# A two-layer decoder on one core: the gate rides in the routed row, the last join is shared by three engines, and four early weight loads are issued between others

## The reference, cut to what matters

```python
logits = xf @ gate_w + gate_b
probs = softmax(logits)
gates, expert_idx = top_k(probs, 2)
h = relu(einsum('nc,ech->neh', xf, w1) + b1)           # 256 -> 512, per expert
expert_out = einsum('neh,ehc->nec', h, w2) + b2        # 512 -> 256
out = sum over a token's two experts of gate * expert_out
x = layernorm(x + out)
```

## Time and profile before

| | us |
|---|---|
| median of 3 runs | 1017.17 |
| lowest and highest | 1013.34, 1018.77 |
| the profiled execution | 1013.71 |
| its span in the trace | 1011.9 |
| PE busy in the span | 896.4 (89%) |
| DVE, ACT, POOL busy | 624.8, 483.8, 282.7 |

### The profile page before, as it was taken

How to read it: one execution, slowest core, us unless ns; L and a number is a source line. 1 busy time by engine, 2 the same in 40 slices (tenths; PEclk the granted TensorE clock), 3 DMA queues, 4 the chain that set the end, 5 groups by cost and what they waited for, 6 DMA issues and landing times.

```text
span 1011.9 us, 20131 instructions
## 1 busy us (share of the span) xinstructions
PE 896.4 (89%) x7498; PEld 717.1 (71%) x7498; DVE 624.8 (62%) x1836; ACT 483.8 (48%) x1123; POOL 282.7 (28%) x432
## 2 busy tenths in 40 slices
PE   3669999999997989999999999999999998698980
PEld 2446778768776757677777878687878897597870
DVE  4999886684663898867746778787543632014006
ACT  2335546344555545464545646644446543243430
POOL 4323322221420344312211333333311322124222
PEclk9679999999998989999999999999999999799995
DMA  9999000000010000000000032213111479797944
GB/s 319 405 324 313 8 1 12 11 2 16 32 32 7 17 27 28 17 6 11 12 11 12 28 111 76 73 38 127 53 58 48 136 220 327 274 345 271 383 186 163
DMA packets 39426, 114.88 MB, mean 114 GB/s; under 512 B 5465, under 2 KB 21601, under 8 KB 38689
## 3 DMA queue, kind: packets, MB, share of 16 engines
q1 hardware_dynamic: 35584, 103.35, 29.6%
q0 software_dynamic: 3744, 10.24, 2.7%
HBM read 99.13 MB, written 37.59 MB: 135 GB/s over the span
## 4 chain that ended last, share of the span: by engine, by line
PE 67%; DVE 14%; ACT 5%; DMA 5%; issue 5%; SPq 2%; POOL 1%; POOLq 0%; ACTq 0%; DVEq 0%
PE ps L693 47%; PE ps L698 8%; PE ps L705 6%; PE ps L769 3%; DMA xs_d<-X,idx 2%; ACT PT L1415 1%; DVE PT L1097 1%; DMA EW<-moe_w 1%; ACT slot_rows L1415 1%; PE ps L836 1%; DVE stat L1033 1%; DVE slot_rows L1338 1%; PE ps L994 1%; PE ps L870 1%; DMA slot_rows<-ys_d 1%
## 5 line engine op out<-in xcount | busy, mean ns | idle before, releaser
L1586 POOL TENSOR_TENSOR stat<-stat,mhalf 128x1 f32<-128x1 f32 x112 | 65.7, 586 | 305.6 <-DVE stat L1035 305.5
L693 PE MATMUL ps<-wall,slot_rows 128*128 128x256 f32 (+1 forms) x448 | 134.7, 427 | 10.0 <-ACT KB L1442 8.5
L693 PEld LDWEIGHTS ps<-wall,slot_rows 128*128 128x128 f32 x448 | 79.3, 194 | 32.7 <-issue 21.3
L1097 DVE TENSOR_REDUCE PT<-ps 128x8 f32<-128x1024 f32 x64 | 75.3, 1219 | 24.5 <-PE ps L705 24.5
L705 PEld LDWEIGHTS ps<-KB 32*128 32x128 f32 (+1 forms) x2048 | 66.0, 193 | 27.7 <-issue 22.7
L705 PE MATMUL ps<-KB 32*128 32x128 f32 (+1 forms) x2048 | 78.3, 290 | 8.2 <-ACT slot_rows L1415 3.5
L698 PE MATMUL ps<-cst,PT 128*128 128x128 f32 x512 | 74.2, 281 | 10.4 <-DVE PT L1097 4.1
L693 PE MATMUL ps<-wgu,slot_rows 128*128 128x352 f32 x256 | 79.4, 463 | 1.7 <-ACT PT L1420 0.8
L693 PE MATMUL ps<-slot_rows,wall 128*128 128x128 f32 x640 | 78.3, 277 | 0.3 <-DVE slot_rows L1107 0.2
L693 PEld LDWEIGHTS ps<-slot_rows,wall 128*128 128x128 f32 x640 | 74.9, 192 | 3.9 <-DVE PT L1097 0.8
L698 PEld LDWEIGHTS ps<-cst,PT 128*128 128x128 f32 x512 | 59.4, 144 | 25.2 <-issue 12.7
(11 more groups left out here) (219 smaller groups left out, 1834.3 us busy)
## 6 DMA issues: line engine op xcount, KB each, us to landing
EW<-moe_w SPq DMA_DIRECT2D x30, 514.0 KB, 4.6
EW<-moe_w SPq DMA_DIRECT2D x30, 512.0 KB, 5.4
PT<-moe_w SPq DMA_DIRECT2D x12, 514.0 KB, 6.2
PT<-moe_w SPq DMA_DIRECT2D x12, 512.0 KB, 7.7
wall<-wts SPq DMA_DIRECT2D x1, 4104.0 KB, 20.0
work<-xs_d SPq DMA_DIRECT2D x31, 128.5 KB, 4.1
slot_rows<-ys_d SPq DMA_DIRECT2D x8, 384.0 KB, 8.6
KB<-ys_d SPq DMA_DIRECT2D x8, 384.0 KB, 6.5
```

The source lines that it names most:

```text
L693: last = k.e.matmul(o, a, b, start=(i == 0), stop=(i == len(pairs) - 1))
L1097: e.tensor_reduce(peak[:, 2 * p:2 * p + 2, :, DH], s4, AX.X, ALU.max).then_inc(emptied[u.at], 1)
L1586: return k.e.tensor_tensor(v[:, 7:8], v[:, 8:9], mhalf[:, :], ALU.pow)
```

## The change

**Gate.** A row gets a 258th number, the gate of that expert. DVE writes the first gate and POOL the first place (a new copy ahead of the first scatter, with a semaphore wait); POOL rewrites both ahead of the second. In a tile's turn ACT copies the column of gates to `gate8`, and the copy of the down result out of PSUM becomes an activation with that column as its scale. What comes back in `ys_d` is already multiplied.

**Join.** POOL adds the first result to the record's third part ("add", one sample ahead), DVE adds the second and takes the statistics, with one more instruction that negates the mean, ACT adds the negated mean, POOL does the power, and ACT multiplies.

**Plan.** An early load of tile x needs the up load of tile x-5 first. The planner is told of 12 us more for each fetch of batch 0, of the new costs, and that rows wait for ACT's part of a turn (`gated`).

```diff
-XW = D + 1
+XW = D + 2
+def lead(x):
+    return x - 5
 def plan_tiles(turns=tile_turns):
-            last = {"rows": [("f", "M", "xT", y), ("M", "placed", y)], ...
+            last = {"rows": [("M", "xT", y), ("M", "placed", y)], ...
-                        needs=[("table", b), *[(n, "sent") for n in BATCHES[b]], *last * (y is not None)])
+                        needs=[("table", b), *[(n, "sent") for n in BATCHES[b]], *last * (y is not None),
+                               *[("load up", lead(x))] * early(what, x)])
-            yield piece(0.3, [xT], [("d", 0.15, ("M", "placed", x)), ("A", 0.37, xT)],
+            yield piece(0.3, [xT], [("d", 0.15, ("M", "placed", x)), ("A", 0.57, xT)],
 def join_turns():
         yield from (("fetch", n) for n in samples)
+        yield "add", samples[0]
         for n in samples:
+            if n < samples[-1]:
+                yield "add", n + 1
             yield "join", n
 def plan_join():
-            yield piece(work=[..., ("L", 2.4, (n, "fetched"))],
+            yield piece(work=[..., ("L", 2.4 + 12.0 * early_one, (n, "fetched"))],
-            yield piece(work=[("D", 1.75, None), ("P", 0.57, (n, "last root"))], needs=[(n, "fetched")], alone=True)
+            yield piece(work=[("D", 1.4, None), ("a", 0.4, None), ("P", 0.57, (n, "last root"))], needs=[(n, "halved")],
+                        alone=True)
+        elif what == "add":
+            yield piece(work=[("P", 0.75, (n, "halved"))], needs=[(n, "fetched")], alone=True)
         def dve_router(k):
-                e.tensor_copy(X6[:, slot(n), D:XW], k_("dest")[:, 2 * n:2 * n + 1])
+                e.tensor_copy(X6[:, slot(n), D + 1:XW], mx8[:, n, 0:1])
         def dve_join(k):
-                    k.wait_ge(fetched[n], 16)
-                    for i in range(2):
-                        e.scalar_tensor_tensor(out=x6, in0=rows_[:, i * D:(i + 1) * D], scalar=mx8[:, n, i:i + 1], in1=x6,
-                                               op0=ALU.mult, op1=ALU.add).then_inc(joined, 1)
-                        k.wait_ge(joined, 2 * n + i + 1)
-                    dve_stats(k, v, x6, 1e-5).then_inc(var6, 1)
-                elif what == "finish":
-                    k.wait_ge(root6, n + 1)
-                    e.tensor_scalar(x6, x6, v[:, 6:7], v[:, 7:8], ALU.subtract, ALU.mult).then_inc(out_ready, 1)
+                    k.wait_ge(halved, n + 1)
+                    e.tensor_tensor(x6, x6, rows_[:, D:2 * D], ALU.add).then_inc(joined, 1)
+                    k.wait_ge(joined, n + 1)
+                    k.after(k.step(e.bn_stats(v[:, 0:6], x6)))
+                    k.after(k.step(e.bn_aggr(v[:, 6:8], v[:, 0:6])))
+                    e.tensor_scalar(v[:, 8:9], v[:, 7:8], 1e-5, None, ALU.add).then_inc(var6, 1)
+                    e.tensor_scalar(v[:, 6:7], v[:, 6:7], -1.0, None, ALU.mult).then_inc(var6, 1)
+        def act_join(k):
+                if what == "join":
+                    k.wait_ge(var6, 2 * n + 2)
+                    k.e.activation(x6, x6, ACT.Identity, scale=1.0, bias=v[:, 6:7]).then_inc(centred, 1)
+                elif what == "finish":
+                    k.wait_ge(centred, n + 1)
+                    k.wait_ge(root6, n + 1)
+                    k.e.activation(x6, x6, ACT.Identity, scale=v[:, 7:8], bias=0.0).then_inc(out_ready, 1)
         def act_tiles(k):
+                    i, y, uses = HOME["rows"][x]
+                    k.wait_ge(ld_xs[i], 16 * uses)
+                    k.e.copy(gate8[:, x % 8:x % 8 + 1], XS[i][:, D + 1:XW]).then_inc(gated, 1)
                     act_copy(k, M["xT", x], XST[x % 2])
-                    k.e.copy(YB[i], ps[:, u.at, 0:D]).then_inc(emptied[u.at], 1)
+                    k.wait_ge(gated, x + 1)
+                    k.e.activation(YB[i], ps[:, u.at, 0:D], ACT.Identity, scale=gate8[:, x % 8:x % 8 + 1],
+                                   bias=0.0).then_inc(emptied[u.at], 1)
         def pool_router(k):
+                k.e.tensor_copy(X6[:, slot(n), D:D + 1], k_("dest")[:, 2 * n:2 * n + 1]).then_inc(directed, 1)
+                k.wait_ge(directed, n + 1)
         def pool_join(k):
+                if what == "add":
+                    k.wait_ge(fetched[n], 16)
+                    k.e.tensor_tensor(x6, x6, rows_[:, 0:D], ALU.add).then_inc(halved, 1)
+                elif what == "join":
+                    k.wait_ge(var6, 2 * n + 2)
+                    pool_root(k, mv2[:, n % 8, :]).then_inc(root6, 1)
```

38 lines of the change are left out of this document (22 added, 16 removed).

## The result

| | before | after |
|---|---|---|
| median, lowest to highest (20 runs each) | 1017.59, 1011.65 to 1022.29 | 1010.23, 1006.76 to 1016.16 |
| ratio after / before, 95% interval | | 0.9937, 0.9924 to 0.995 |
| the profiled execution and its span | 1013.71, 1011.9 | 1011.70, 1009.8 |

What follows compares the result with a forecast made beforehand. PE, busy 896.4 of 1011.9 us, was taken as the bound, with transfers nearly full from 850 to 970. Gains 6 + (7.8 - 2.5) + 2 - 1 = 12.3 from 1015.4 gave 1003 us, range 993 to 1012.

Steps and rivals of the forecast that it cites:

- early loads: Early weight pairs spread among batch 0's loads: up(23) starts about 6 us earlier, bounds 3.5 to 10.
- joins of batch 0: Places of tiles 29 to 31 ahead of the joins: 7.8 us gained, less 2.5 for work on POOL and ACT.
- joins of batch 1: Eight joins at the end, 17.45 us, shared by three engines: gain 2, bounds a loss of 1 to a gain of 3.6.
- new order in the attention stage: Four more ACT table loads and 16 POOL waits: a loss of 1 us, bounds -3 and +20.
- copies of gates and places: Tile part: 46 one-column ACT copies hidden, at most 19 us uncovered; POOL's new copies were counted only around the last scatters.
- What then decides is the sum of bytes: Behind 858 us, 7.7 MB up to tile 22's down half take 19 us at 404 GB/s; up(23) starts at about 880.7.
- The first step: Early loads: SP issues the up half of tile 20 at 858 us, 3.6 us earlier.
- rival "half": Early pairs still ahead of batch 0's halves, or joins hold ACT by 4 us: gain 5 to 10 us, chance 0.20.
- rival "slower": Planner's rewritten order from 590 to 855 us loses 20 us of PE: about 1022 us, chance 0.07.
- The sign to watch: Sign that the prediction is wrong: PE busy under 95% from 590 to 855 us.
- One of my signs: Sign that the prediction is right: no block of 16 us between two places on DVE.
- DVE's add waits out the power in every other join: SBUF port conflict with POOL in joins: adds 0.34 us to POOL's 1.41, giving a step of 1.75.

Runs made afterwards that it cites:

- e1: Kernel before with ACT's part of a turn planned at 0.57 us in place of 0.37; 1020.0 us, ratio 1.0028.
- e13: Changed kernel with ACT's part of a turn planned at 0.37 us again, a repeat of e2; 1007.6 us, ratio to before 0.9903.
- e2: Changed kernel with ACT's part of a turn planned at 0.37 us again, all instructions kept; 1006.5 us, ratio to before 0.9900.
- e3: Kernel before with the early loads alone spread out (tile x needs the up load of tile x-5); 1014.4 us, ratio 0.9968.
- e18: e2 with early pairs 25 and 26 behind batch 0's loads, early rows of tiles 23 and 24 behind pair 24; 1005.4 us, ratio to before 0.9902.
- e6: Changed kernel with ACT's part of a turn planned at 0.60 us in place of 0.57; 1013.5 us, ratio to before 0.9964.
- e7: Changed kernel with ACT's part of a turn planned at 0.70 us in place of 0.57; 1008.7 us, ratio to before 0.9917.
- e12: Changed kernel with both adds of a join on DVE and, in the tail, an unread two-input POOL add per join; 1012.5 us, single run.
- e16: e2 with the early pair of tile 26 tied to the up load of tile 22; 1006.4 us, ratio to before 0.9888.
- e11: e2 with each early pair tied to the up load of tile x-4 in place of x-5; 1008.3 us, ratio to before 0.9888.

## Where the prediction failed and where it held, step by step

| term of the sum | forecast | shown |
|---|---|---|
| early loads | 6 | 3.3, 2.4 and 0.9 in three pairs of kernels; 0.8 to 2.8 from the last router matmul to up(23) |
| joins of batch 0 | 7.8 - 2.5 | 7.9 (94.6 to 86.7) |
| joins of batch 1 | 2 | 4.3 (17.45 to 13.2), 3.1 to 4.3 over all kernels |
| new order in the attention stage | -1 | -2.9 (e1), -3.5 and -3.8 (against e13, e2) |
| copies of gates and places | 0 | about -1.1, ahead of the mark |

**The step that failed most is "What then decides is the sum of bytes".** I let the last half of tile 22 land when 7.7 MB had passed, at 878.5, and so gave 22.7 us from the issue of tile 20's up half to up(23). These 22.7 us were mis-sized: they are 25.3 before (861.62 to 886.92), 29.7 after the change (867.36 to 897.07) and 30.5 in e3. More bytes passed in that time than I had counted: 9.2 MB (867.36 to 890.77, 395 GB/s), transfers issued earlier and some behind the last halves among them. And two things that I left out held the last halves: a half can't be issued until its home is free, and then it can stand in SP's queue behind an early pair that nobody needs yet. The first step held: by the marks the up half of tile 20 goes out 6.5 us earlier in e3 than before, where I had said 3.6. The rival "half" described this (early pairs ahead of batch 0's halves in smaller pieces, waits of 1 to 2 us and slow ups after them), and it came to pass: 1.25, 2.46, 1.30 and 4.08 us, and 16 matmuls of an up in 3.51. Its gain of 5 to 10 us holds the measured one too. The SP wait that I did see, the store behind the first pair, was real too: the up half of tile 20 went out 1.1 us after the store. The gain of about 6 can be had, but by another order (e18: 5.5 at up(23)).

**The second is "I take a loss of 1" for the rewritten order.** The mechanism is that of the rival "slower", at a seventh to a fifth of its 20 us. My cost of it was four table loads; e6 and e7 show that they don't decide. The sign to watch, PE under 95% from 590 to 855, was blind: PE was at 97.7%.

**The joins of batch 0** went as told, and the 2.5 us against them never came. PE waited for no rows, and 0.5 us for ACT, which was at 26.9 of 40 us from 905 to 945. This term came out 2.5 us better than I forecast and the tail 1 to 2, which hid part of the loss in the other terms; that the time still fell in the range owes something to this luck. One of my signs was badly chosen: from the place at 911.28 to the next at 927.58 there are still 16.3 us, but three tiles later, where they hold nobody.

**The tail** was mis-sized by the port: the 4.3 us lie outside my bound of 3.6. "DVE's add waits out the power in every other join" did not happen in the tail, as the row at 994.26 shows. Without these 0.34 us my own sum is a step of 1.41, and 1.39 was measured. The Trainium skill (SBUF — State Buffer, "Who interferes with whom") lets a DVE instruction with two SBUF inputs contend with a GpSimd instruction that reads SBUF. For a full-size add the runs agree (0.95 in e12). For a power of 128x1 they are divided: 0.42 three times in the tail, 0.76 and 0.70 in the joins of batch 0. My rows 10 held no power at all, so I had carried the rule from an add to it.

**Hidden work** was hidden behind the mark: up to the last router matmul e2, with all copies of gates and places, takes 237.2 us for 236.9. Ahead of the mark it was not. The new copy of the first place (L1732) and its wait move POOL's work, and at 291.37 an add of DVE that took 0.95 before takes 2.01, with POOL's power, add and products beside it. First before, then after the change:

```profile
288.53 0.95 DVE L1084 TENSOR_TENSOR PT<-slot_rows,cst 128x256 f32<-128x256 f32 x1
```

```profile
291.37 2.01 DVE L1098 TENSOR_TENSOR PT<-slot_rows,cst 128x256 f32<-128x256 f32 x1
```

```profile
289.33 0.18 POOL L1732 COPY X<-cst 128x1 f32<-128x1 f32 x1
289.81 1.07 POOL L1734 DMA_INDIRECT xs_d<-X,idx  x1 [0.29 <-POOL X L1732]
290.91 0.64 POOL L1615 TENSOR_TENSOR stat<-stat,mhalf 128x1 f32<-128x1 f32 x1
291.53 0.71 POOL L1699 TENSOR_TENSOR slot_rows<-slot_rows 128x256 f32<-128x256 f32 x1
292.21 0.85 POOL L1639 TENSOR_TENSOR Y<-slot_rows,cst 128x128 f32<-128x128 f32 x2
```

The add takes 2.01 or 2.02 us in all fifteen kernels with the new instructions and 0.94 or 0.95 in all five without. PE stands still behind it for 2.40 us in the fifteen and for 1.34 in e1; in the other four the matmuls ahead ran slowly (3.3 to 3.6 us for 1.9) and covered the wait. That is about 1.1 us (2.40 less 1.34) for a term that I had put at nothing. The rows look like the earlier trace rows, the conflict that I had looked for in the tail.

With it the terms shown (about 2 + 7.9 + 4.3 - 3.5 - 1.1 = 9.6) still exceed the measured 7.4; the two traces give 8.6 from the mark on. The entry into the mark varied from 600.3 to 606.3 us among all profiles but that of before, by the speed of the matmuls (PE busy 535.7 to 540.1 us up to there) and by PE's idle time (62.7 to 66.2). The rest stays open.

**The best versions** are the changed kernel with the turn planned at 0.37 again: 0.9900 and 0.9903 as it is, 0.9888 (0.9867 to 0.9909) with e16's edit, 0.9888 (0.9858 to 0.9918) with e11's and 0.9902 (0.9877 to 0.9926) with e18's, all faster than both kernels, and none of them told from another. By the marks of one execution e18 is 3 us ahead of e2 (399.8 for 402.8); its time does not show that.

## What to carry to other kernels

When a planner or a scheduler sets the order, find which edit rewrites it and keep that edit apart: here a cost set closer to the trace (0.57 for a copy and a turn) gave an order worse by 3 to 4 us, and undoing it was the cheapest gain of the study. Compare stages between instructions that are the same in both kernels, not between clock times and not by busy share. When loads are moved ahead, follow the last load that the stage needs: when its buffer is free, and what stands ahead of it in the queue; the first one says little. And a small instruction on an engine that has time to spare moves all the work behind it; look for what that work then runs beside.
